# Global attention with the value product in fp32: probabilities and values no longer split into fp16 halves, V transposed in fp32, split projection weights in two buffers

## What is computed

```python
def proj(W, bias):
    y = jnp.tanh(states @ W + bias)
    return y.reshape(b, s, h, d).transpose(0, 2, 1, 3)
q, k, v = (proj(Wq, bq), proj(Wk, bk), proj(Wv, bv))
alpha = jnp.einsum('bhqd,bhkd->bhqk', q, k) / jnp.sqrt(jnp.float32(d))
alpha = jnp.where(causal, alpha, jnp.finfo(jnp.float32).min)
alpha = jax.nn.softmax(alpha, axis=-1)
ctx = jnp.einsum('bhqk,bhkd->bhqd', alpha, v)
ctx = ctx.transpose(0, 2, 1, 3).reshape(b, s, h * d)
return jnp.tanh(ctx @ Wo + bo)
```

## Time and profile before

| | |
|---|---|
| median of 3 runs | 2997.27 us (2996.97 to 2999.57) |
| span of the profiled execution, its own time | 2999.0 us |
| TensorE busy | 2509.8 us, 84% |
| VectorE busy | 2103.4 us, 70% |
| ACT busy | 1630.0 us, 54% |
| GpSimd busy | 864.7 us, 29% |
| mean granted TensorE clock | 0.949 |
| attention, first and last context transposition | 140.4 and 1168.2 us |

### The profile page before, as it was taken

One profiled execution on the slowest core, in us unless ns is written; L12 is line 12 of the kernel. 1 busy time (PEld: TensorE's weight loads), 2 busy tenths in 40 slices (PEclk: granted clock), 3 DMA queues, 4 the chain that ended last, 5 costly groups with the idle time before them and its releaser, 6 DMA issues. The chain is left out here.

```text
span 2999.0 us, 68027 instructions
## 1 busy us (share of the span) xinstructions
PE 2509.8 (84%) x22296; PEld 1960.9 (65%) x22296; DVE 2103.4 (70%) x4501; ACT 1630.0 (54%) x3100; POOL 864.7 (29%) x732
## 2 busy tenths in 40 slices
PE   5699989989998998188998895799698989894996
PEld 3466656666666666177777774688577777773885
DVE  5588668858885885667777775566577777774656
ACT  2566556646664674356666664333466666662332
POOL 0233223313331332333333332111233333332111
PEclk7899999999999999599999998899899999997998
DMA  4400020010002000400000000100100000000003
GB/s 154 143 11 16 5 73 11 13 65 14 13 10 68 11 15 19 140 1 0 7 1 6 4 3 6 45 0 0 34 0 7 0 7 0 7 0 7 0 0 112
DMA packets 74546, 77.26 MB, mean 26 GB/s; under 512 B 4224, under 2 KB 67320, under 8 KB 72952
## 3 DMA queue, kind: packets, MB, share of 16 engines
q1 hardware_dynamic: 74488, 76.46, 7.8%
HBM read 55.48 MB, written 16.78 MB: 24 GB/s over the span
## 5 line engine op out<-in xcount | busy, mean ns | idle before, releaser
L501 ACT ACTIVATE at_p<-at_ps_s,at_shift 128x1024 f32<-128x1024 f32 (+3 forms) x384 | 343.0, 902 | 112.1 <-DVE at_p_lo L435 50.3
L74 PE MATMUL ly_ps<-ly_w_hi,ly_operands 128*128 128x256 f32 (+1 forms) x1048 | 372.6, 356 | 33.6 <-DVE ly_operands L1221 17.2
L435 DVE TENSOR_TENSOR at_p_lo<-at_p,at_p_hi 128x1024 f16<-128x1024 f32 (+3 forms) x384 | 391.4, 1019 | 12.1
L1018 ACT ACTIVATE ly_probs<-ly_masked,ly_small,ly_rq 128x256 f32<-128x256 f32 x512 | 303.5, 594 | 145.2 <-DVE ly_small L1206 145.0
L431 DVE CAST at_p_hi<-at_p 128x1024 f16<-128x1024 f32 (+3 forms) x384 | 283.0, 737 | 140.9 <-PE at_ps_o L569 100.9
L75 PE MATMUL ly_ps<-ly_w_lo,ly_operands 128*128 128x256 f32 (+1 forms) x1048 | 347.4, 332 | 0.0
L76 PE MATMUL ly_ps<-ly_w_hi,ly_operands 128*128 128x256 f32 (+1 forms) x1048 | 346.5, 331 | 0.0
L567 PE MATMUL at_ps_o<-at_v,at_p_hi 128*128 128x65 f16 x2304 | 249.5, 194 | 36.0 <-DVE at_p_lo L435 36.0
L567 PEld LDWEIGHTS at_ps_o<-at_v,at_p_hi 128*128 128x128 f16 x2304 | 209.6, 96 | 99.9 <-DVE at_p_lo L435 56.1
L1417 PEld LDWEIGHTS ly_ps<-ly_values,ly_probs_T 128*128 128x128 f32 x2048 | 258.5, 191 | 12.3 <-issue 0.8
L1417 PE MATMUL ly_ps<-ly_values,ly_probs_T 128*128 x2048 | 256.7, 268 | 0.0
(11 more groups left out here) (208 smaller groups left out, 6331.1 us busy)
## 6 DMA issues: line engine op xcount, KB each, us to landing
at_hT<-hT_hi SPq DMA_DIRECT2D x5, 1024.0 KB, 5.0
at_hT<-hT_lo SPq DMA_DIRECT2D x5, 1024.0 KB, 8.1
at_w_raw<-in_Wv SPq DMA_DIRECT2D x34, 128.0 KB, 2.1
at_w_raw<-in_Wq SPq DMA_DIRECT2D x34, 128.0 KB, 2.3
at_w_raw<-in_Wk SPq DMA_DIRECT2D x34, 128.0 KB, 2.3
n_x<-in_states SPq DMA_DIRECT2D x4, 1024.0 KB, 11.6
hT_hi<-n_hi SPq DMA_DIRECT2D x8, 512.0 KB, 3.0
hT_lo<-n_lo SPq DMA_DIRECT2D x8, 512.0 KB, 3.1
```

The costliest lines, as they stand in the source:

```text
L74: pe.matmul(out, w_hi, x_hi, start=first, stop=False, skip_group_check=True)
L435: dve.tensor_tensor(p_lo[u % 2][:, :, off:], probs[u % 2][:, :, off:], p_hi[u % 2][:, :, off:], ALU.subtract).then_inc(p_lo_done, 1)
L501: act.activation(probs[u % 2][:, :, off:], ps_s[u % 2][:, :, off:], ACT.Exp, bias=shift[:], scale=SCORE_SCALE).then_inc(exp_done, 1)
L1018: step = act.activation(pr[:, j % 2, h, :], sm[:, j % 2, h, :], ACT.Exp, bias=small[:, j % 2, 1, h:h + 1], scale=rq[:, par, 2 * j + h:2 * ...
```

## The change

The value product becomes one fp32 matmul of 65 columns for each tile and head, on the probabilities as the exponential writes them, in three buffers (`P_RING`). The casts and subtractions on VectorE go, and so does the constant that was added to the exponent. V goes through tanh once, in fp32; eight fp32 transpositions, four for each half of the tokens and into one PSUM tile each, replace sixteen of fp16, and VectorE copies both results (`copy_values`). GpSimd subtracts for Q and K only. The split weights `at_w_hi` and `at_w_lo` have two buffers; ACT splits at unit 5 instead of 11, and VectorE between the first normalisation and the first context half. The projection of K's second half moves from step 10 to behind the last value product of the iteration; the first context transpositions move from step 11 to step 8. Q, K, the scores, the output projection and all other phases stay as they are.

```diff
 LAG = 2
+P_RING = 3
-FIRST_PROJ = 4
-PROJ_AT = {1: 0, 2: 1, 6: 2, 7: 3, 9: 4, 10: 5}
+NQK = 4
+BANK = (0, 1, 0, 1, 1, 0)
+PROJ_AT = {1: 0, 2: 1, 6: 2, 7: 3, 9: 4, NU + LAG - 1: 5}
 VALUES_AT = {3: 0, 4: 1}
-CTX_AT = 11
+SPLIT_AT = 5
+CTX_AT = 8
...
-        w_hi = a.sb("at_w_hi", [P, 3, KT, P], F32R)
-        w_lo = a.sb("at_w_lo", [P, 3, KT, P], F32R)
+        w_hi = a.sb("at_w_hi", [P, 2, 3, KT, P], F32R)
+        w_lo = a.sb("at_w_lo", [P, 2, 3, KT, P], F32R)
...
-        vT = [a.sb(f"at_vT_{part}", [P, S], F16) for part in ("hi", "lo")]
-        v = [a.sb(f"at_v{i}", [P, TB, 2, VW], F16) for i in range(2)]
-        probs = [a.sb(f"at_p{i}", [P, 2, CH]) for i in range(2)]
-        p_hi = [a.sb(f"at_p_hi{i}", [P, 2, CH], F16) for i in range(2)]
-        p_lo = [a.sb(f"at_p_lo{i}", [P, 2, CH], F16) for i in range(2)]
+        vT = a.sb("at_vT", [P, S])
+        v = [a.sb(f"at_v{i}", [P, TB, 2, DH + 1]) for i in range(2)]
+        probs = [a.sb(f"at_p{i}", [P, 2, CH]) for i in range(P_RING)]
...
+                def copy_values(n, c, dst):
+
+                    dve.wait_ge(vt_mm, NC * n + c + 1)
+                    dve.tensor_copy(v[dst][:, c * CT:(c + 1) * CT, :, 0:DH],
+                                    ps_m[c][:].rearrange("p (t h d) -> p t h d", h=2, d=DH)).then_inc(v_done, 1)
...
-                            for u, (qc, kt) in enumerate(UNITS):
-                                off = max(0, kt * P - qc * CH)
-                                dve.wait_ge(exp_done, at(it * NU + u + 1))
-                                dve.wait_ge(pv_done, at(it * NU + u - 1))
-                                dve.tensor_copy(p_hi[u % 2][:, :, off:], probs[u % 2][:, :, off:]).then_inc(p_hi_done, 1)
-                                if u == CT - 1 + LAG:
-                                    normalise(it * NC, it * NU + CT)
-                                dve.wait_ge(p_hi_done, at(it * NU + u + 1))
-                                dve.tensor_tensor(p_lo[u % 2][:, :, off:], probs[u % 2][:, :, off:],
-                                                  p_hi[u % 2][:, :, off:], ALU.subtract).then_inc(p_lo_done, 1)
-                                if VALUES_AT.get(u) == 1:
-                                    low_values(it + 1, 1 - par)
-                                if u == CTX_AT:
-                                    low_context(it * NC, hp, 0)
+                            for c in range(NC):
+                                copy_values(it + 1, c, 1 - par)
+                            normalise(it * NC, it * NU + CT)
+                            split_weights(it + 2, par)
+                            low_context(it * NC, hp, 0)
                             normalise(it * NC + 1, it * NU + NU)
-                            split_weights(it + 2)
                             low_context(it * NC + 1, hp, 1)
...
                                 act.wait_ge(sc_done, it * NU + u + 1)
-                                act.wait_ge(p_lo_done, at(it * NU + u - 1))
-                                act.activation(probs[u % 2][:, :, off:], ps_s[u % 2][:, :, off:], ACT.Exp,
-                                               bias=shift[:], scale=SCORE_SCALE).then_inc(exp_done, 1)
+                                act.wait_ge(pv_done, at(it * NU + u + 1 - P_RING))
+                                act.activation(probs[u % P_RING][:, :, off:], ps_s[u % 2][:, :, off:], ACT.Exp,
+                                               scale=SCORE_SCALE).then_inc(exp_done, 1)
...
+                            project(it + 1, PROJ_AT[NU + LAG - 1], (hp + 1) % HP, 1 - par)
                             high_context(it * NC + 1, hp, 1)
...
-                        ones_hi, lo = v[par][:, kt, h, 0:DH + 1], v[par][:, kt, h, DH + 2:VW]
                         for t in range(first, CT):
-                            ph, pl = (p[u % 2][:, h, t * P:(t + 1) * P] for p in (p_hi, p_lo))
-                            out = ps_o[:, h, t * (DH + 1):(t + 1) * (DH + 1)]
-                            pe.matmul(out, ph, ones_hi, start=(kt == 0 and t == 0), stop=False, skip_group_check=True)
-                            pe.matmul(out[:, 0:DH], ph, lo, start=False, stop=False, skip_group_check=True)
-                            step = pe.matmul(out, pl, ones_hi, start=False, stop=(kt == qc * CT + t), skip_group_check=True)
+                            step = pe.matmul(ps_o[:, h, t * (DH + 1):(t + 1) * (DH + 1)],
+                                             probs[u % P_RING][:, h, t * P:(t + 1) * P], v[par][:, kt, h, :],
+                                             start=(kt == 0 and t == 0), stop=(kt == qc * CT + t), skip_group_check=True)
...
-                                    pe.wait_ge(p_lo_done, at(it * NU + u + 1))
+                                    pe.wait_ge(exp_done, at(it * NU + u + 1))
                                     value_products(par, u)
-                            pe.wait_ge(pj_lo, at(base + FIRST_PROJ))
-                            pe.wait_ge(exp_done, at(it * NU + NU - 1))
+                            pe.wait_ge(ct_lo, at(it * NC + 1))
+                            project(PROJ_AT[NU + LAG - 1], buf, 1 - par)
+                            pe.wait_ge(pj_lo, at(qbase + 2))
                             scores(1 - par, 0)
-                            pe.wait_ge(pj_hi, at(base + NPJ))
+                            pe.wait_ge(pj_hi, at(qbase + 3))
                             context(it * NC + 1, 1)
```

More of the change, by code:

```diff
@@ L457, in _, with split_weights, project @@
             def _(act):
-                for s in (exp_done, pj_full, pj_hi, vt_hi, ct_hi, y_done, wh_done):
+                for s in (exp_done, pj_full, v_full, pj_hi, ct_hi, y_done, wh_done):
                     act.sem_inc(s, CREDIT)
[L461 to L466, removed]
+                def split_weights(n, slot, projected):
+                    hold(act, tick, (ld_w, 48 * n + 48), (pj_mm, at(projected)))
+                    act.activation(w_hi[:, slot], w_raw[:], ACT.Copy).then_inc(wh_done, 1)
+                def project(n, i, hp, dst):
                     w, c = PROJ[i]
[L469 to L472, removed]
+                    if w == V_:
+                        hold(act, tick, (pj_mm, at(NPJ * n + i + 1)))
+                        act.activation(vT[:, c * CH:(c + 1) * CH], ps_m[BANK[i]][:], ACT.Tanh,
+                                       bias=bias[:, w, ds(hp, 1)]).then_inc(v_full, 1)
+                        return
+                    q = NQK * n + i - 2
+                    hold(act, tick, (pj_mm, at(NPJ * n + i + 1)), (pj_lo, at(q - 1)))
+                    act.activation(stage[:, i % 2, :], ps_m[BANK[i]][:], ACT.Tanh, bias=bias[:, w, ds(hp, 1)]).then_inc(pj_full, 1)
+                    act.activation(qk[dst][w - 1][0][:, c * CH:(c + 1) * CH], ps_m[BANK[i]][:], ACT.Tanh,
                                    bias=bias[:, w, ds(hp, 1)]).then_inc(pj_hi, 1)
-                def high_values(n, dst):
-                    act.wait_ge(vt_mm, 2 * n + 1)
-                    act.activation(v[dst][:, :, :, 0:DH], ps_m16[1], ACT.Copy).then_inc(vt_hi, 1)
                 def high_context(n, hp, c):
@@ L527, in project, with values @@
                     for k in range(KT):
-                        step = three_products(pe, ps_m[i % 2][:], w_hi[:, w, k, :], w_lo[:, w, k, :],
+                        step = three_products(pe, ps_m[BANK[i]][:], w_hi[:, slot, w, k, :], w_lo[:, slot, w, k, :],
                                               hT[:, buf, 0, k, cols], hT[:, buf, 1, k, cols], k == 0, k == KT - 1)
                     step.then_inc(pj_mm, 1)
-                def values(part, base):
-                    pe.wait_ge(pj_lo if part else pj_hi, at(base + NC))
-                    for t in range(TB):
-                        step = pe.transpose(ps_m16[1 - part][:, t, :, :].rearrange("p h d -> p (h d)"),
-                                            vT[part][:, t * P:(t + 1) * P], ident16[:])
+                def values(n, c):
+                    pe.wait_ge(v_full, at(NC * n + c + 1))
+                    for t in range(CT):
+                        step = pe.transpose(ps_m[c][:, t * P:(t + 1) * P],
+                                            vT[:, (c * CT + t) * P:(c * CT + t + 1) * P], ident[:])
                     step.then_inc(vt_mm, 1)
@@ L589, in _ @@
                 pe.wait_ge(wl_done, at(1))
-                for i in range(NPJ):
-                    if i >= 2:
-                        pe.wait_ge(pj_hi, at(i - 1))
-                    project(i, 0)
+                project(0, 0, 0)
+                project(1, 0, 0)
+                values(0, 0)
+                values(0, 1)
+                for i in range(2, NPJ):
+                    if i < 4:
+                        pe.wait_ge(v_done, at(i - 1))
+                    elif i == 4:
+                        pe.wait_ge(pj_hi, at(2))
+                    project(i, 0, 0)
                 pe.wait_ge(ld_const, 16 * 4)
-                pe.wait_ge(pj_hi, at(NPJ))
```

(19 more changed lines are left out.)

80 lines of the change are left out of this document (27 added, 53 removed).

## The result

The changed kernel takes 3164.17 us (median of 4, 3163.41 to 3166.12) against 2998.42 before (4 runs): a ratio of 1.055, 95% interval 1.0535 to 1.0564, so 5.5% slower.

A forecast was written before the change was run, and what follows sets the result against it. TensorE, stalled in a loop with VectorE, was taken as the bound. Projections 8.9, scores 8.0, transpositions 0.9 and 0.9, value products 17.3 and stalls 0.3 gave 36.3 us an iteration: 197 us over 32, so 3196, range 3166 to 3230.

The forecast's parts named there:

- TensorE's own list: In the attention iteration, TensorE's projections, scores, transpositions and value products sum to 36.0 us, plus 0.3 for small stalls.
- The first rival (loads hide): Value products: weight loads hide, 0.056 us a record, an iteration of 28.25 us and 2938 in all; 4 in 100.
- the second (one record): Value products: each fp32 product is one record, like the transpositions, so 9.1 us an iteration and 2932; 2 in 100.
- the third (ACT paces): Attention iteration: waits for ACT bring back stalls of 3.7 us, so 39.7 us an iteration and 3305; 5 in 100.
- value products: Per attention iteration: 144 records at 0.112 us plus 1.2 for unit ends, 17.3 us in place of 7.8.
- Small stalls: TensorE's remaining waits in an attention iteration, taken at 0.3 us.
- 6.15 x 32: Whole attention phase: each of 32 iterations grows from 30.15 to 36.3 us, 197 us in all.
- lower bound for a record, 0.105: Value products: 0.105 us a record instead of 0.112 would take 32 us off the forecast.
- The width hardly matters: Value products: 65 columns in place of 64 cost nothing, read from L247's 0.21 us a record with 4 columns.
- Exp without the added shift costs the same: ACT's exp in the attention phase: leaving out the shift changes its time by nothing.
- an iteration early: SP's reload of the one raw weight buffer after both splits, with two split buffers: taken to cost nothing.
- the old stalls are VectorE's: Kernel before: TensorE and VectorE hold each other up through exp, cast, subtract, product and release; 3.7 us an iteration.

The follow-up runs named there:

- experiment 3: The changed kernel, with SP loading the raw weights one iteration earlier: 3161.58 us, 2.6 less than the changed kernel.
- experiment 5: The kernel before without casts and subtractions of the probabilities, written in fp16 into three buffers; all three products read that tile: 2935.85 us, ratio 0.9785.
- experiment 7: The kernel before with one fp16 value product of three, casts and subtractions on VectorE kept: 2980.18 us, ratio 0.9936.
- experiment 1: The changed kernel with probabilities and V in fp32r instead of fp32, the product 66 columns wide: 2924.68 us, ratio 0.9752.
- experiment 4: The changed kernel's schedule with the old three fp16 products, their casts and subtractions and the exponent's shift: 3051.68 us, ratio 1.0163.
- experiment 8: The kernel before with the exponent's constant shift left out: 2994.82 us, ratio 0.9987.
- experiment 2: The changed kernel with fp32r probabilities and V, and the raw weights loaded one iteration earlier: 2902.53 us, ratio 0.9676.
- experiment 6: The changed kernel with the old schedule and one buffer of split weights: 3171.87 us, ratio 1.0568.

## Why the prediction missed its range

**Right:** that TensorE's own list becomes the iteration; two records a product, 4608 in all; 0.112 us from one to the next; VectorE's and ACT's savings hidden. The first rival (loads hide) is excluded by the gaps of 0.112, the second (one record) by the count, the third (ACT paces) by 1.7 us of waits for ACT in the whole phase.

**The first step that failed, a term of the sum:** *value products* were taken at 17.3 us an iteration and are 16.6. The prediction counted all 144 records at 0.112 and 12 unit ends at 0.10, although its own row showed a burst that opens with a gap of 0.056. In the trace an iteration has ten bursts, since the last three units run as one. Seven of them, behind a projection or transpositions, open with 0.056 to 0.061; the two behind a mask open with 0.112, and one behind scores with 0.161. The short openings give 0.3 us and the ends 0.4. A full unit with a short opening is 16 x 0.112 + 0.10 - 0.056 = 1.84, and 1.83 was measured. *Small stalls* of 0.3 did not come; projections took 9.1 instead of 8.9 and transpositions 1.9 instead of 1.8. Together that is 35.6 us in place of 36.3, -0.7, or 22 us in all.

**The second step that failed:** the whole difference, "6.15 x 32", is laid on 32 iterations alike, the three that hold a batch boundary among them. Their intervals were to grow by an iteration's 5.5 us as all others, and grew from 60.5, 59.6 and 59.6 to 62.2, 61.2 and 61.5: some 3.8 us each less, 11 in all. There the kernel before waited 2.9 to 3.3 us for instructions, 9.3 in sum, and had 13.7 us at half the clock; the changed kernel has neither, and pays some 2.8 for its late weights (experiment 3). How much of the 11 is the clock's was not measured apart. The change shortens TensorE's code for two iterations from 728 matmuls to 424 (568 records), and the wait is gone; experiments 5 and 7 show that the length decides. The four output projections (22.55 us each before, 22.56 after) and the layers (1808 us from the last of them to the end in both) did stay. The waits on issue stood in the trace of before; the prediction read only the undisturbed stretch. 197 - 22 - 11 = 164, and the two spans differ by 165.3 us.

Either miss alone would have left the time inside the range, at 3174 or 3185. The prediction's own lower bound for a record, 0.105, gave 3196 - 32 = 3164; the range was cut above it, at 3166.

**Steps wrong without weight in the sum.** "The width hardly matters" was read from records of 4 columns 0.21 us apart. That is nearly twice 0.112, so this row can't carry it; the conclusion held all the same (experiment 1). "Exp without the added shift costs the same": it is 0.09 us shorter. And the raw weights, "an iteration early", at no cost: at a batch start they come 6.9 us late for ACT, which costs 2.6 us here (experiment 3) and 22 where products are short. That the old stalls are VectorE's, in a loop of cast, subtract and product, was right for 2.0 of 3.7 us (experiment 5).

## What to carry to other kernels

Price a matmul by the gap between records of the same kind of operands, and count the records, not the calls: here fp32 cost two of 0.112 us, fp32r one, and three fp16 products 0.09 together. Here the split that kept VectorE busy for 25 of 30 us was no waste, since the product that does without it costs TensorE 8.8 us more (16.6 against 7.8) and gives back 3.7 us of stalls. With one record a product (fp32r) removing the split wins, at a lower precision. Read the stretches where the loops turn as well as the steady ones: code length and late loads showed there alone.

## What the runs showed of the hardware

**Instruction fetches.** In the kernel before and in experiments 4, 5 and 8 TensorE has 712 or 728 matmul records in two iterations, which are the body of the inner loop. Each of these traces has 40 fetches, which go on through all four batches, and 2.9 to 3.5 us of waiting at each boundary. With 568 records or fewer (the changed kernel, experiments 1, 2, 3, 6 and 7) there are 11 or 12 fetches, at most one of them between the first batch boundary and the end of the attention phase, and no such wait. The Trainium skill (Advanced Engine Details and Errata, ISA Cache) gives TensorE 128 KB in lines of 16 KB, 256 instructions each; 0.66 MB in 40 fetches agree with the line, and no run here measures the whole.

**VectorE and GpSimd take turns.** In the kernel before (timelines of VectorE and of GpSimd), a subtraction of 768 columns that starts inside one of GpSimd's ends 0.82 us after that has ended and takes 1.80, where one that starts ahead of GpSimd's takes 0.96. And where VectorE is first, GpSimd's takes 2.15 us:

```profile
451.24 1.80 DVE L435 TENSOR_TENSOR at_p_lo<-at_p,at_p_hi 128x768 f16<-128x768 f32 x1
...
450.81 1.41 POOL L378 TENSOR_TENSOR at_vT_lo<-at_stage,at_vT_hi 128x512 f16<-128x512 f32 x1 [6.82 <-ACT at_vT_hi L472]
...
469.75 0.96 DVE L435 TENSOR_TENSOR at_p_lo<-at_p,at_p_hi 128x768 f16<-128x768 f32 x1
...
462.10 1.23 DVE L435 TENSOR_TENSOR at_p_lo<-at_p,at_p_hi 128x1024 f16<-128x1024 f32 x1
...
462.20 2.15 POOL L378 TENSOR_TENSOR at_q1lo<-at_stage,at_q1hi 128x512 f16<-128x512 f32 x1 [8.14 <-ACT at_q1hi L472]
```

In the changed kernel the same subtraction on GpSimd takes 1.16 us:

```profile
L374 POOL TENSOR_TENSOR at_q0lo<-at_stage,at_q0hi 128x512 f16<-128x512 f32 x6 | 7.0, 1159 | 61.3 <-ACT at_q0hi L465 61.3
```

The Trainium skill (SBUF — State Buffer, Terms) says that the two share a port pair that one holds for its full instruction; these rows agree. It may be part of why the iterations stayed at 30 us in experiment 7, where VectorE's subtractions of 768 columns took 1.63 us on the mean; no run tested that.
